# A recommender tower on one core: the products inside two quads joined as sixteen tiles of 32 by 32, and the sums' bank from the common ring

## The chip, the cores and the metric

The kernel runs on one core of a Trainium2 chip. The metric is the device time in microseconds of one execution. A run of the kernel gives one time; the number before the change is the median of three runs.

## What is computed

For each of 512 samples, forty embedding rows of 32 numbers are looked up in forty tables (1,000 to 125,000 rows). Every pair of fields i < j gives one number z = v_i . W_ij . v_j, with a 32 by 32 matrix for each of the 780 pairs. The 780 numbers and 16 context numbers go through three dense layers (796 to 512 to 256 to 1). All is float32.

```
vi = embeddings[:, _I_IDX, :]
vj = embeddings[:, _J_IDX, :]
z = jnp.einsum('bke,kef,bkf->bk', vi, W, vj)
h = jnp.concatenate([z, dense_ctx], axis=1)
h = jnp.maximum(h @ W_top1 + b_top1, 0.0)
h = jnp.maximum(h @ W_top2 + b_top2, 0.0)
y = h @ W_top3
```

## The kernel before

The forty fields stand in ten quads of four fields; a quad fills 128 partitions (four slots of 32), with the 512 samples along the free axis: `emb[:, q, :]`. Quads 0, 1, 3 and 5 ("hot") have small tables. They are looked up on TensorE: ids are spread over the partitions (`spread`, L554), one-hots are made by VectorE (L485) or ScalarE (L405, L408), and multiplied with the table in three bf16 pieces (L572). The other six are gathered by POOL with 96 indirect DMAs (L381), 16 a quad, and turned by TensorE (`turn`, L585). ScalarE copies each finished quad to `emb` (`land`, L415 and L418).

A group (slots, stream) joins two quads. TensorE multiplies each slot's 32 rows of the stream quad with the weights of its four pairs (`map_group`, L600). For two different quads (45 cross groups) these are four row groups of 32, each with two column halves of 64: 8 products of 32 by 64, that go to four banks, a bank for each row group. A group inside one quad (ten) has 4 products of 64 by 64 into two banks. Every float32 product is two instructions, so 16 and 8. Two banks of results are one operation; there are 100 operations, two for each cross group and one for each group inside a quad. An operation is multiplied with the slots' quad, two banks at a time (`multiply`, L316): by VectorE straight from PSUM, or, if it is in COPIED_OPS, from a copy that ScalarE makes (L429), or, if it is in POOL_OPS, by POOL from such a copy. The results go to a ring of eight in SBUF (`prod`). For two operations at a time, TensorE adds up the 32 partitions of each slot with a selector (`sum_ops`, L617): four column groups of 32 with four different streams, 8 instructions, into one bank, `z_ps`. Sixteen operations fill a z tile, which ScalarE copies to `zt` (`save_z`, L433); the sums of the next tile wait for that copy. There are seven z tiles. The first dense layer is added up in parts (`layer1`, L626) as z tiles are ready, its last part, the second layer (L667) and the third (L673) are the tail.

PSUM has eight banks: seven in a ring (`ring_ps`), one for `z_ps`. Orders are written out by hand as strings, one letter a step. TENSOR_ORDER: i spread, l look-up, t turn, m map group, s sum, 1 dense layer. VECTOR_ORDER: r pieces of a table, o one-hot, w multiplication, a addition of a dense part. SCALAR_ORDER: I ids to 16 bits, o one-hot, L landing of a quad, c copy, z copy of a z tile, 1 dense part. BANKS has a digit for each use of the ring, in TensorE's order; a pair is that bank and the next. Before a step, TensorE waits until the last users of its banks are done (`banks_free`). POOL's own queue holds the 96 gathers and then its multiplications.

Of the kernel before, what the change touches and what calls it, by code (L numbers as in the profile page):

```python
# [23 lines left out]
ALU = mybir.AluOpType  # L24
# [26 lines left out]
def quads():  # L51
# [3 lines left out]
    for vocab in HOT_VOCABS:  # L55
# [17 lines left out]
GROUPS = [(slots, stream) for stream in range(QUADS) for slots in range(stream + 1)]  # L73
PAIRS_WITHIN = [(1, 0), (2, 0), (3, 1), (0, 3), (1, 2), (2, 3)]
OPS = [(g, half) for g, (slots, stream) in enumerate(GROUPS) for half in range(1 if slots == stream else 2)]
NOPS = len(OPS)
OPS_OF = [[o for o, (of, _) in enumerate(OPS) if of == g] for g in range(len(GROUPS))]
# [10 lines left out]
RING_BANKS = 7  # L88
# [12 lines left out]
TENSOR_ORDER = ("iillllllilllilllllmllmmtlllmlsllslmlllmmssmsmmstslmlllmlslmlllmmlsmssmssmstmsmsmm1mssmssm1mstmmsmssm"  # L101
                "1msmsm1mstmsmmssmssm1mssm1mssm1mtmmssmssm1mssmssms1m11msssmm1s")


BANKS = ("0240624304042065202024024024660240240240240206420242064024026403042402460242026406204024020640241422"
         "4642604204246024024604320402462301")

VECTOR_ORDER = ("rooooorooooooooooroowwwwooowworwwwwwwwwwooowwwowowwwwwwwwwwwwwwwwwwwwwwwwwwwwwwwwwwwwwwwwwwwwwwwwwww"
                "wwwawwwwaawwwwwawwwwwwwaawawwwa")


SCALAR_ORDER = ("IIoIIIIILIoLoLooLooLooozLcccLzc1cLcc1zc1c1ccLcczcccccLcccczcccczc")
# [47 lines left out]
def bank_users():  # L160
# [597 lines left out]
```

## Time and profile before

| | us |
|---|---|
| median of three runs | 187.92 (187.42 to 188.01) |
| the profiled execution, its own time | 187.37 |
| its span, first to last instruction | 185.6 |
| TensorE busy | 173.7 |
| VectorE busy | 148.1 |
| POOL busy | 114.6 |
| ScalarE busy | 91.9 |

The profiled execution took 1.8 us more than its span. A busy time is the time in which at least one instruction of the engine ran. The pieces of the chain of waits cut TensorE's overlapping instructions at the start of the next piece, so they add up to the time that passes.

### The profile page before, as it was taken

The page shows a single profiled execution, that of the slowest core. Times are in us where ns is not written, and L with a number is a line of the kernel's source. Part 1 is how long each engine was busy: PE and PEld are TensorE (multiplying, and loading weights), DVE is VectorE, ACT ScalarE, POOL GpSimd, SP SyncE. Part 2 cuts the span into 40 slices and gives each one's busy share as a digit, 9 for nine tenths or more (in the row PEclk, how much of TensorE's full clock was granted, in tenths as well). Part 3 has the DMA queues.
Part 4 walks back from the last instruction along what each step waited for, and adds up shares of the span by engine and source line. Part 5 has one row for each costly group of instructions (what it writes and reads, how often), then busy time and mean ns, then how long its engine had stood idle before and what let it go on. Part 6 is the DMA issues. An engine that isn't in the chain of part 4 may idle for free.

```text
span 185.6 us, 4607 instructions
## 1 busy us (share of the span) xinstructions
PE 173.7 (94%) x1976; PEld 47.5 (26%) x1976; DVE 148.1 (80%) x141; ACT 91.9 (50%) x83; POOL 114.6 (62%) x107
## 2 busy tenths in 40 slices
PE   2899979998999999999999899999999899999993
PEld 0243323321333222122221122222221122223331
DVE  0999979998999788997898989888957859981500
ACT  4966999979599521530351533432453342130511
POOL 2877877787877777787777878788096370531000
PEclk9999999999999999999999999999999999999999
DMA  5999400000000019500100000000000000000000
GB/s 173 374 395 359 168 14 16 14 14 14 16 14 16 18 24 350 175 12 11 18 13 16 14 15 15 11 14 14 4 4 0 4 0 4 0 0 4 0 4 0
DMA packets 7212, 10.80 MB, mean 58 GB/s; under 512 B 2052, under 2 KB 4744, under 8 KB 7192
## 3 DMA queue, kind: packets, MB, share of 16 engines
q1 hardware_dynamic: 4088, 8.89, 13.2%
q0 software_dynamic: 3072, 1.58, 4.8%
q8 instruction: 16, 0.26, 0.6%
q10 hardware_dynamic: 32, 0.03, 0.1%
q14 instruction: 4, 0.03, 0.1%
HBM read 10.50 MB, written 0.00 MB: 57 GB/s over the span
## 4 chain that ended last, share of the span: by engine, by line
PE 85%; DVE 5%; ACT 5%; issue 2%; DMA 2%; SPq 0%; DVEq 0%; ACTq 0%
PE ring_ps L600 31%; PE z_ps L617 22%; PE ring_ps L626 14%; PE ring_ps L572 12%; PE ring_ps L667 4%; DVE prod L316 3%; DMA table<-hot_table 2%; ACT copied L429 2%; PE ring_ps L585 2%; ACT distance L405 1%; PE ring_ps L554 1%; ACT one_hot L408 1%; DVE rest L471 1%; DVE one_hot L485 0%; ACT h L463 0%
## 5 line engine op out<-in xcount | busy, mean ns | idle before, releaser
L381 POOL DMA_INDIRECT rows<-table,idx x96 | 97.8, 1019 | 31.7 <-issue 28.9
L316 DVE TENSOR_TENSOR prod<-ring_ps,emb 128x1024 f32<-128x1024 f32 x73 | 86.8, 1219 | 12.1 <-PE ring_ps L600 11.4
L600 PE MATMUL ring_ps<-emb,wall 32*64 32x512 f32 (+1 forms) x800 | 60.6, 612 | 4.4 <-DVE prod L316 2.5
L429 ACT ACTIVATE copied<-ring_ps 128x1024 f32<-128x1024 f32 x27 | 27.6, 1024 | 54.7 <-PE ring_ps L600 51.8
L617 PE MATMUL z_ps<-prod,consts_sb 128*32 128x512 f32 x400 | 49.9, 600 | 0.1
L316 DVE TENSOR_TENSOR prod<-copied,emb 128x1024 f32<-128x1024 f32 x20 | 26.5, 1330 | 5.0 <-ACT copied L429 5.0
L316 POOL TENSOR_TENSOR prod<-copied,emb 128x1024 f32<-128x1024 f32 x7 | 16.6, 2375 | 21.2 <-ACT copied L429 21.2
L626 PE MATMUL ring_ps<-zt,w_sb 128*32 128x512 f32 x224 | 26.7, 597 | 0.0
L600 PEld LDWEIGHTS ring_ps<-emb,wall 32*64 32x64 f32 (+1 forms) x800 | 12.9, 130 | 44.4 <-issue 22.4
L405 ACT ACTIVATE distance<-ids,vocab 128x2048 f16<-128x2048 f16 x10 | 20.0, 2000 | 0.8 <-PE ring_ps L572 0.2
L408 ACT ACTIVATE one_hot<-distance,vocab 128x2048 bf16<-128x2048 f16 x10 | 20.0, 2003 | 0.3
L617 PEld LDWEIGHTS z_ps<-prod,consts_sb 128*32 128x32 f32 x400 | 9.8, 108 | 34.3 <-issue 20.1
L485 DVE TENSOR_SCALAR one_hot<-ids,vocab 128x2048 bf16<-128x2048 f16 x26 | 17.9, 745 | 0.0
L572 PE MATMUL ring_ps<-one_hot,table 128*32 128x512 bf16 x144 | 14.9, 403 | 0.6 <-DVE one_hot L485 0.6
L572 PE MATMUL ring_ps<-one_hot,rest 128*32 128x512 bf16 x144 | 14.9, 400 | 0.0
L572 PE MATMUL ring_ps<-one_hot,third 128*32 128x512 bf16 x144 | 14.8, 398 | 0.0
L626 PEld LDWEIGHTS ring_ps<-zt,w_sb 128*32 128x32 f32 x224 | 6.6, 109 | 18.5 <-issue 16.1
L393 ACT ACTIVATE ids<-ring_ps 128x1024 f16<-128x1024 f32 x8 | 7.8, 1019 | 4.4 <-PE ring_ps L554 4.4
L554 PE MATMUL ring_ps<-ids_rows 16*128 16x512 f16 x16 | 5.8, 500 | 3.7 <-ACT ids_rows L444 3.5
L471 DVE TENSOR_TENSOR rest<-table 128x1024 f32<-128x1024 f32 (+1 forms) x4 | 5.4, 1351 | 4.8 <-DMA table<-hot_table 4.8
L433 ACT ACTIVATE zt<-z_ps 128x512 f32<-128x512 f32 x6 | 3.6, 595 | 7.5 <-PE z_ps L617 7.5
L572 PEld LDWEIGHTS ring_ps<-one_hot,table 128*32 128x32 bf16 x144 | 4.1, 100 | 12.5 <-issue 5.3
(25 smaller groups left out, 56.4 us busy)
## 6 DMA issues: line engine op xcount, KB each, us to landing
w_sb<-w SPq DMA_DIRECT2D x4, 512.0 KB, 5.1
rows<-table,idx POOLq DMA_INDIRECT x96, 2.3
table<-hot_table SPq DMA_DIRECT2D x2, 640.0 KB, 5.9
table<-hot_table SPq DMA_DIRECT2D x2, 512.0 KB, 3.8
wall<-w_pairs SPq DMA_DIRECT2D x1, 640.0 KB, 11.3
wall<-w_pairs SPq DMA_DIRECT2D x1, 576.0 KB
wall<-w_pairs SPq DMA_DIRECT2D x1, 512.0 KB, 8.4
wall<-w_pairs SPq DMA_DIRECT2D x1, 448.0 KB
```

The lines of the kernel that those rows point to most:

```text
L316: return eng.tensor_tensor(prod[:, o % RING_P], products, emb[:, slots:slots + 1, :].to_broadcast([P, 2, BATCH]), ALU.mult)
L381: nc.gpsimd.indirect_dma_start(rows[:, k, c, r, :], None, tables[f], bass.IndirectOffsetOnAxis(ap=idx[:, c, f:f + 1], axis=0)).then_inc(ga ...
L393: nc.scalar.activation(ids16[:, h, 2 * half:2 * half + 2, :], pair(("spread", h), half), ACT.Copy).then_inc(ids16_done, 1)
L405: nc.scalar.activation(distance[:], ids16[:, h].rearrange("p r b -> p (r b)"), ACT.Abs, bias=vocab_column(h, t, -1)).then_inc(distance_don ...
L408: nc.scalar.activation(one_hot[:, n % RING_ONE_HOT, :], distance[:], ACT.Relu, bias=vocab[:, 4 * MAX_TILES:], scale=-1.0).then_inc(one_hot ...
L429: nc.scalar.activation(copied_op(o), op_banks(o), ACT.Copy).then_inc(copied_ready, 1)
L485: nc.vector.tensor_scalar(one_hot[:, n % RING_ONE_HOT, :], ids16[:, h].rearrange("p r b -> p (r b)"), vocab_column(h, t), None, ALU.is_equ ...
L554: mm = nc.tensor.matmul(pair(("spread", h), r // 2)[:, r % 2, :], column, ids_rows[:, :BATCH], start=True, stop=True)
L572: mm = nc.tensor.matmul(bank(("hot", (h, 0)))[DIM * r:DIM * (r + 1), :], shaped[:, r, t, :], one_hot[:, n % RING_ONE_HOT, r * BATCH:(r + 1 ...
L600: mm = nc.tensor.matmul(pair(("map", g), i // 2)[half, i % 2, :], wall[own, g, half], emb[own, stream, :], start=True, stop=True)
L617: mm = nc.tensor.matmul(z_ps[DIM * g:DIM * (g + 1), :], sel[:, m, :], prod[:, t // 2 % RING_P, t % 2, :], start=m == 0, stop=last)
L626: mm = nc.tensor.matmul(bank[DIM * c:DIM * (c + 1), :], w1_sb[:, k, first:first + DIM], zt[:, k, :], start=start and k == ks[0], stop=stop ...
```

## The change

The ten groups inside a quad become five, each for two neighbouring quads (0 and 1, 2 and 3, and so on), with stream = the second one. A joined group has two operations, one for each quad, so 100 operations stay; each operation has two banks of four blocks of 32 by 32, six of them pairs and two with zero weights. All sixteen blocks of a joined group have their own place in the array; a bank takes blocks from two to four row groups. The joined group waits for both quads. The group (0, 0), which only needed quad 0, is gone, so the first map group is (0, 1). The weights' load for stream 0 is gone too (`load_weights`), and those that follow bring only what is left, 50 groups instead of 55.

The separate bank of the sums becomes the eighth of the ring. Each z tile takes a bank by its own digit in BANKS, and its first sum waits for that bank's last user; whoever takes a z tile's bank later waits for its copy to `zt`. Pairs have a digit for each bank now and need not be neighbours.

The four orders, the banks, and the lists of operations on POOL (four instead of seven), of copies (20 as before, beside POOL's) and of ScalarE's one-hots (ten as before) are new.

```diff
-GROUPS = [(slots, stream) for stream in range(QUADS) for slots in range(stream + 1)]
-PAIRS_WITHIN = [(1, 0), (2, 0), (3, 1), (0, 3), (1, 2), (2, 3)]
-OPS = [(g, half) for g, (slots, stream) in enumerate(GROUPS) for half in range(1 if slots == stream else 2)]
+GROUPS = [(slots, stream) for stream in range(1, QUADS) for slots in range(stream + stream % 2)]
+BLOCKS_WITHIN = [[[(0, 0), (1, 0), (2, 0), (3, 1)], [(0, 3), (1, 2), (2, 3), (3, 3)]],
+                 [[(0, 1), (1, 3), (2, 2), (3, 0)], [(0, 2), (1, 1), (2, 1), (3, 2)]]]
+OPS = [(g, half) for g in range(len(GROUPS)) for half in range(2)]
 NOPS = len(OPS)
-OPS_OF = [[o for o, (of, _) in enumerate(OPS) if of == g] for g in range(len(GROUPS))]
+OPS_OF = [[2 * g, 2 * g + 1] for g in range(len(GROUPS))]
...
-RING_BANKS = 7
+RING_BANKS = 8
...
-TENSOR_ORDER = ("iillllllilllilllllmllmmtlllmlsllslmlllmmssmsmmstslmlllmlslmlllmmlsmssmssmstmsmsmm1mssmssm1mstmmsmssm"
-                "1msmsm1mstmsmmssmssm1mssm1mssm1mtmmssmssm1mssmssms1m11msssmm1s")
-
-
-BANKS = ("0240624304042065202024024024660240240240240206420242064024026403042402460242026406204024020640241422"
-         "4642604204246024024604320402462301")
-
-VECTOR_ORDER = ("rooooorooooooooooroowwwwooowworwwwwwwwwwooowwwowowwwwwwwwwwwwwwwwwwwwwwwwwwwwwwwwwwwwwwwwwwwwwwwwwww"
-                "wwwawwwwaawwwwwawwwwwwwaawawwwa")
-
-
-SCALAR_ORDER = ("IIoIIIIILIoLoLooLooLooozLcccLzc1cLcc1zc1c1ccLcczcccccLcccczcccczc")
-
-POOL_OPS = [77, 78, 80, 85, 87, 93, 98]
-COPIED_OPS = [28, 32, 34, 37, 45, 47, 48, 54, 56, 60, 62, 64, 67, 69, 73, 75, 81, 84, 89, 92]
-SCALAR_ONE_HOTS = [4, 17, 21, 23, 25, 27, 30, 31, 34, 35]
+TENSOR_ORDER = ("iiillllllillllllllllmmtsllmlllmlllllsmssmsmsmtllmlssmlllmlllssmlsmsmsmsmsmtsmm1mssmssmsmtsm1mssm1mmm"
+                "ssm1mssmtsmssmssm1mssm1m1mstmssm1mssmmsm1sms1mssms1mssm1s")
+
+
+BANKS = ("0123456701235670142345670132534670134670145670145670135346701346701734012345014523450145230164523670"
+         "1345672014567014501745673014567015236701456723501674672301237670123674012375601235670156723017562301"
+         "6750123236701457234560123601452345601234501762345")
+
+VECTOR_ORDER = ("rooooooooroooooooorowwwoowowowwwrwwwwwwowoowwwowowwwwwwwwwwwwwwwwwwwwwwwwwwwwwwwwwwwwwwwwwwwwwwwwwww"
+                "wawawwawwwwwwawwwwwwwawwwwawwawwwa")
+
+
+SCALAR_ORDER = ("IIIoIIIoLoLIILooLooLooozLcccLzcccL1z11ccccc1LzcccLcccczccccccz")
+
+POOL_OPS = [74, 85, 93, 94]
+COPIED_OPS = [25, 27, 29, 35, 36, 43, 53, 55, 56, 59, 61, 73, 76, 77, 78, 80, 83, 87, 88, 90]
+SCALAR_ONE_HOTS = [4, 10, 16, 20, 25, 26, 27, 33, 34, 35]
...
+def slots_quad(o):
+
+    g, half = OPS[o]
+    slots, stream = GROUPS[g]
+    return stream - 1 + half if within(g) else slots
...
-        if kind == "sum" or kind == "hot" and what[1]:
+        if kind == "sum":
+            if what % GROUP:
+                continue
+            step = "z", what // GROUP
+        if kind == "hot" and what[1]:
             continue
-        size = 2 if kind in ("spread", "map") else 1
-        uses = 2 if kind == "spread" else len(OPS_OF[what]) if kind == "map" else 1
-        banks[step] = [digits.pop(0) for _ in range(uses)]
-        own = [(i, bank) for i, low in enumerate(banks[step]) for bank in range(low, low + size)]
-        before[step] = list(dict.fromkeys(last[bank] for _, bank in own if bank in last))
-        for i, bank in own:
-            last[bank] = (step, i)
+        banks[step] = [digits.pop(0) for _ in range(2 * 2 if kind in ("spread", "map") else 1)]
+        before[step] = list(dict.fromkeys(last[bank] for bank in banks[step] if bank in last))
+        for i, bank in enumerate(banks[step]):
+            last[bank] = (step, i // 2)
...
-            return ring_ps[:, banks[step][i]:banks[step][i] + 2, :]
+            first, second = banks[step][2 * i:2 * i + 2]
+            return ring_ps[:, first:second + 1:second - first, :]
...
-            load_weights(0)
...
-                nc.scalar.activation(zt[:, k, :], z_ps[:], ACT.Copy).then_inc(z_saved, 1)
+                nc.scalar.activation(zt[:, k, :], bank(("z", k)), ACT.Copy).then_inc(z_saved, 1)
...
+                    elif kind == "z":
+                        pe.wait_ge(z_saved, what + 1)
...
-                    pe.wait_ge(landed, landings(stream))
+                    pe.wait_ge(landed, max(landings(q) for q in range(stream + 1)))
                 banks_free(("map", g))
-                height = P // 2 if slots == stream else DIM
-                for i in range(P // height):
-                    own = slice(height * i, height * (i + 1))
+                if within(g):
+                    for half in range(2):
+                        for i, blocks in enumerate(BLOCKS_WITHIN[half]):
+                            for s, r in blocks:
+                                to, own = slice(DIM * s, DIM * (s + 1)), slice(DIM * r, DIM * (r + 1))
+                                mm = nc.tensor.matmul(pair(("map", g), half)[to, i, :], wall[own, g, to],
+                                                      emb[own, stream - 1 + half, :], start=True, stop=True)
+                        mm.then_inc(mapped, 1)
+                    return
+                for i in range(SLOTS):
+                    own = slice(DIM * i, DIM * (i + 1))
                     for c in range(2):
-                        half = slice(P // 2 * c, P // 2 * (c + 1))
-                        mm = nc.tensor.matmul(pair(("map", g), i // 2)[half, i % 2, :], wall[own, g, half],
+                        to = slice(P // 2 * c, P // 2 * (c + 1))
+                        mm = nc.tensor.matmul(pair(("map", g), i // 2)[to, i % 2, :], wall[own, g, to],
                                               emb[own, stream, :], start=True, stop=True)
                     if i % 2:
...
-                    if t % ZTILE == 0 and k:
-                        pe.wait_ge(z_saved, k)
+                    if t % ZTILE == 0:
+                        banks_free(("z", k))
                     last = m == GROUP - 1 or t >= TILES - SLOTS
-                    mm = nc.tensor.matmul(z_ps[DIM * g:DIM * (g + 1), :], sel[:, m, :],
+                    mm = nc.tensor.matmul(bank(("z", k))[DIM * g:DIM * (g + 1), :], sel[:, m, :],
```

## Rows read from the trace of the kernel before

**Rows 1.** Totals of the page: busy time, share of the span, instructions.

```profile
span 185.6 us, 4607 instructions
PE 173.7 (94%) x1976; PEld 47.5 (26%) x1976; DVE 148.1 (80%) x141; ACT 91.9 (50%) x83; POOL 114.6 (62%) x107
```

**Rows 2.** The chain of waits, shares of the span by engine and by line.

```profile
PE 85%; DVE 5%; ACT 5%; issue 2%; DMA 2%; SPq 0%; DVEq 0%; ACTq 0%
PE ring_ps L600 31%; PE z_ps L617 22%; PE ring_ps L626 14%; PE ring_ps L572 12%; PE ring_ps L667 4%; DVE prod L316 3%; DMA table<-hot_table 2%; ACT copied L429 2%; PE ring_ps L585 2%; ACT distance L405 1%; PE ring_ps L554 1%; ACT one_hot L408 1%; DVE rest L471 1%; DVE one_hot L485 0%; ACT h L463 0%
```

**Rows 3.** Stretches: length, busy us of PE, PEld, DVE, ACT, POOL, granted clock, DMA.

```profile
24.92:64.00 39.08, 38.12 (x517) 11.78 (x519) 35.75 (x35) 34.33 (x21) 30.10 (x30) 1.00 0.08 15
64.00:136.00 72.00, 70.88 (x781) 16.14 (x781) 64.65 (x56) 23.14 (x27) 52.28 (x51) 1.00 0.17 46
136.00:169.00 33.00, 31.73 (x344) 7.59 (x340) 23.99 (x21) 11.81 (x13) 15.08 (x7) 1.00 0.00 1
```

**Rows 4.** Groups by line, shapes apart: count, busy us, mean ns, idle before.

```profile
L316 DVE TENSOR_TENSOR prod<-ring_ps,emb 128x1024 f32<-128x1024 f32 x73 | 86.8, 1219 | 12.1 <-PE ring_ps L600 11.4 <-ACT emb L415 0.3 <-PE z_ps L617 0.3
L617 PE MATMUL z_ps<-prod,consts_sb 128*32 128x512 f32 x400 | 49.9, 600 | 0.1
L316 DVE TENSOR_TENSOR prod<-copied,emb 128x1024 f32<-128x1024 f32 x20 | 26.5, 1330 | 5.0 <-ACT copied L429 5.0
L600 PEld LDWEIGHTS ring_ps<-emb,wall 32*64 32x64 f32 x720 | 10.8, 129 | 37.3 <-issue 19.4 <-DVE prod L316 13.7 <-ACT copied L429 4.2
```

**Rows 5.** Pieces of the chain of waits: start us, us, what, instructions.

```profile
81.91 1.85 PE z_ps L617 x16
...
90.60 1.00 PE z_ps L617 x8
...
92.18 2.06 PE ring_ps L600 x24
...
95.25 1.04 PE ring_ps L600 x16
```

**Rows 6.** Timeline (start, us, what): a cross group's weight loads; three multiplications.

```profile
66.86 0.23 PEld L600 LDWEIGHTS ring_ps<-emb,wall 32*64 32x64 f32 x16 [0.84 <-DVE prod L316]
...
26.14 3.49 DVE L316 TENSOR_TENSOR prod<-ring_ps,emb 128x1024 f32<-128x1024 f32 x3 [1.07 <-PE ring_ps L600]
```

**Rows 7.** Timeline of the first stage: ScalarE, TensorE and SP's queue.

```profile
4.53 1.94 ACT L393 ACTIVATE ids<-ring_ps 128x1024 f16<-128x1024 f32 x2 [1.12 <-PE ring_ps L554]
6.57 2.00 ACT L405 ACTIVATE distance<-ids,vocab 128x2048 f16<-128x2048 f16 x1
8.61 2.00 ACT L408 ACTIVATE one_hot<-distance,vocab 128x2048 bf16<-128x2048 f16 x1
...
24.20 0.58 ACT L415 ACTIVATE emb<-ring_ps 128x512 f32<-128x512 f32 x1
...
24.92 2.14 PE L600 MATMUL ring_ps<-emb,wall 32*64 32x512 f32 x24 [1.13 <-ACT emb L415]
26.99 0.66 PE L585 MATMUL ring_ps<-consts_sb,rows 128*128 128x128 f32 x4
...
2.61 0.91 SPq L348 DMA_DIRECT2D wall<-w_pairs  x2
```

**Rows 8.** The last gather, the gathers' time to landing, and the last turn.

```profile
129.02 0.95 POOL L381 DMA_INDIRECT rows<-table,idx  x1 [0.30 <-issue]
...
DMA to landing us min/median/max: 2.2/2.3/3.3
...
135.98 0.66 PE L585 MATMUL ring_ps<-consts_sb,rows 128*128 128x128 f32 x4
```

**Rows 9.** Timeline of the end of the steps.

```profile
163.01 2.13 PE L600 MATMUL ring_ps<-emb,wall 32*64 32x512 f32 x24
...
165.42 2.40 POOL L316 TENSOR_TENSOR prod<-copied,emb 128x1024 f32<-128x1024 f32 x1 [4.41 <-ACT copied L429]
...
167.96 1.07 PE L617 MATMUL z_ps<-prod,consts_sb 128*32 128x512 f32 x8
```

More of the change, by code:

```diff
@@ L97, with within @@
 TAIL = (5, 6)
[L101 to L116 removed]
+TENSOR_ORDER = ("iiillllllillllllllllmmtsllmlllmlllllsmssmsmsmtllmlssmlllmlllssmlsmsmsmsmsmtsmm1mssmssmsmtsm1mssm1mmm"
[9 more added lines that the diff above has]
+SCALAR_ONE_HOTS = [4, 10, 16, 20, 25, 26, 27, 33, 34, 35]
+def within(g):
+    slots, stream = GROUPS[g]
+    return slots == stream
+def slots_quad(o):
+    g, half = OPS[o]
+    slots, stream = GROUPS[g]
+    return stream - 1 + half if within(g) else slots
 def z_place(t):
@@ L286, in op_banks @@
             return pair(("map", g), half)
-        others = [i for i in range(RING_BANKS) if i not in [banks["tail", m][0] for m in range(M1)]]
+        taken = [banks["z", ZTILES - 1][0]] + [banks["tail", m][0] for m in range(M1)]
+        others = [i for i in range(RING_BANKS) if i not in taken]
         h2_ps = [ring_ps[:, others[m], :] for m in range(M2)]
@@ L347, in load_weights @@
                 first = GROUPS.index((0, q))
-                sp.dma_start(wall[:, first:first + q + 1, :].rearrange("p g n -> p (g n)"),
-                             w_pairs[:, first * P:(first + q + 1) * P]).then_inc(wload[q], 16)
+                end = first + q + q % 2
+                sp.dma_start(wall[:, first:end, :].rearrange("p g n -> p (g n)"),
+                             w_pairs[:, first * P:end * P]).then_inc(wload[q], 16)
             sp.dma_start(idx[:].rearrange("p c f -> p (c f)"), ids).then_inc(ids_loaded, 16)
@@ L488, in weight_op @@
             def weight_op(o):
-                slots, _ = GROUPS[OPS[o][0]]
-                dve.wait_ge(landed, landings(slots))
+                dve.wait_ge(landed, landings(slots_quad(o)))
                 if o >= RING_P:
@@ L518, in _ @@
             dve.wait_ge(summed, NOPS // 2)
-            nc.vector.tensor_tensor(zt[:, ZTILES - 1, :], z_ps[:], ctx_sb[:], ALU.add).then_inc(last_z_saved, 1)
+            nc.vector.tensor_tensor(zt[:, ZTILES - 1, :], bank(("z", ZTILES - 1)), ctx_sb[:], ALU.add).then_inc(last_z_saved, 1)
             for m in range(M1):
@@ L686, in packed_weights @@
     for g, (slots, stream) in enumerate(GROUPS):
-        of = PAIRS_WITHIN if slots == stream else [(s, r) for s in range(SLOTS) for r in range(SLOTS)]
-        for s, r in of:
-            packed[r, :, g, s] = block(QUAD_FIELDS[slots][s], QUAD_FIELDS[stream][r])
+        if within(g):
+            of = [(stream - 1 + half, stream - 1 + half, s, r) for half in range(2) for blocks in BLOCKS_WITHIN[half]
+                  for s, r in blocks if s != r]
+        else:
+            of = [(slots, stream, s, r) for s in range(SLOTS) for r in range(SLOTS)]
+        for first, second, s, r in of:
+            packed[r, :, g, s] = block(QUAD_FIELDS[first][s], QUAD_FIELDS[second][r])
     return packed.reshape(P, len(GROUPS) * P)
@@ L699, in packed_layer1 @@
             k, col, m = z_place(2 * o + i)
-            if slots == stream:
-                pairs = PAIRS_WITHIN[3 * i:3 * (i + 1)]
+            if within(g):
+                pairs, of = [(s, r) for s, r in BLOCKS_WITHIN[half][i] if s != r], stream - 1 + half
             else:
-                pairs = [(s, 2 * half + i) for s in range(SLOTS)]
+                pairs, of = [(s, 2 * half + i) for s in range(SLOTS)], stream
             for s, r in pairs:
-                a, b = sorted((QUAD_FIELDS[slots][s], QUAD_FIELDS[stream][r]))
+                a, b = sorted((QUAD_FIELDS[slots_quad(o)][s], QUAD_FIELDS[of][r]))
                 packed[k, DIM * col + SLOTS * m + s] = w[pair_index(a, b)]
```

3 lines of the change are left out of this document (1 added, 2 removed).

## The prediction, made before the change was run

> **What bounds the kernel now.** I read the totals first, then the chain of waits, then the pieces of that chain, and last the stretches. The totals show TensorE busy for 173.7 of 185.6 us and VectorE for 148.1 [rows 1]. The chain puts 85% of the span on TensorE and 5% on VectorE; by line, the block products (L600) have 31% and the sums (L617) 22% [rows 2]. So time is won where TensorE's own steps become fewer or shorter, as long as the engines that feed it keep up. By stretches, TensorE is busy 38.12 of 39.08 us from 24.92, 70.88 of 72.00 from 64 and 31.73 of 33.00 from 136, while VectorE has 35.75, 64.65 and 23.99 there, that is 91%, 90% and 73% [rows 3]. VectorE is therefore the next bound, some 10 points behind. Its idle time is mostly TensorE's doing: 11.4 us of waiting for block products [rows 4], which shrinks when TensorE gets faster.
>
> **Part 1: the products inside a quad.** Every f32 product is two instructions. A cross group has 8 products, 16 instructions; they take 1.04 us. A chain piece with 24 instructions, one cross group and one group inside a quad, takes 2.06 us [rows 5]. So a group inside a quad, with half the products, costs 2.06 - 1.04 = 1.02 us: as much as a whole cross group. Two sums in a row are four passes over 512 columns and take 1.85 us, one ahead of another shape 1.00 [rows 5]: 0.85 for the first, so 0.43 a pass and about 0.15 for a change of shape. Either map group is thus two passes plus 0.16 to 0.18 us, however many tiles stand side by side. The change drops ten such groups: -10.2 us.
>
> It adds five groups of 16 products, 32 instructions. No row shows sixteen tiles of 32 by 32. Below, they can't beat two passes, about 1.02 us. Issue adds little: the 16 weight loads of a cross group begin and end within 0.23 us, one lasting 0.129 [rows 4], so they follow each other at (0.23 - 0.13)/15 = 7 ns [rows 6]. Eight more tiles in each pass start 8 x 7 = 56 ns later, and only the last pass shows that fully: 1.04 + 0.06 = 1.10 us. Above, if only eight tiles run at once, there are two more passes: 1.04 + 0.86 = 1.9 us. Rival B has what lies beyond. I take 1.10, because the rows show that each of its ingredients already runs side by side: four row groups at once (the cross groups), and four column groups with four different streams (the sums). 5 x 1.10 = 5.5 us, so part 1 is worth **-4.7 us**; the bounds are -5.1 and -0.7.
>
> **Part 2: the order.** Counting letters, the sums (49 in the order, one in the tail), cross groups (45), look-ups (36), layer-1 steps (12) and turns (6) stay as they were. Three cross groups now directly follow another cross group. Each such pair saves one change of shape: 3 x 0.16 = **-0.5 us**; at worst nothing.
>
> At the start, the third spread goes ahead of the look-ups, into time in which TensorE waits for the first one-hot anyway. The first cross group now needs quads 0 and 1 landed, and the copy of quad 1 stands behind three of ScalarE's one-hots instead of two. From the first id copy at 4.53 us, six id copies at 0.97, three one-hots at 2 x 2.0 and the copy of quad 0 at 0.55 make 4.5 + 5.8 + 12.1 + 0.55 = 23.0; the copy of quad 1 ends at 23.6 and the first cross group starts at about 23.7, where it was 24.92 [rows 7]. Cross and joined group bring the first turn to 23.7 + 1.04 + 1.10 = 25.85 against 26.99 [rows 7]: 1.1 earlier, just what the dropped groups up to there give. The wider issue on SP (the 64 KB load for stream 0 is gone, some 0.45 us of SP's queue [rows 7]) brings later loads forward by that; the look-ups cover that, for the first cross group waits for ScalarE's copy and not for its weights [rows 7]: zero.
>
> **Part 3: VectorE, POOL, ScalarE.** The 100 multiplications stay, but four instead of seven are POOL's, so VectorE gets three more at about 1.14 us (three in a row take 3.49, one 1.22) [rows 4, 6]: +3.4 us on an engine with room. Up to the last turn VectorE has no more to do than before: about 75 of its operations against 77. Behind it, it has some 21 instead of 16, so 23.99 + 5 x 1.14 = 29.7 us in a stretch that I put at 31 us. That is tight, and is rival A. ScalarE copies 24 instead of 27 tiles, off the path, zero; it is 11.81 us busy in those 33 [rows 3], and would have to be three times as slow to matter.
>
> **Part 4: the sums' bank.** Before, the first sum of a z tile waits for the copy of the last one out of the only bank; now it waits for whoever had its new bank. The waiting instruction holds TensorE's queue, so all later products stand behind it. All 400 instructions of the sums together stood only 0.1 us behind an idle TensorE [rows 4], so the gain is zero. The cost could be a late bank: the ring has eight, the sums hold one, so seven are left, as now. Pairs need no longer be neighbours, so fewer waits, if any. Zero, with half a microsecond on both sides. VectorE reads two banks with a gap between them; its 1.219 us for neighbours and 1.330 us for a copy in SBUF [rows 4] are the nearest bounds (the second would be +0.1 on each of 76, mostly hidden). I take no change: same elements, two runs of 512.
>
> **The gathers.** POOL issues them as before, and the last begins at 129.02 and lands 2.3 us later, at 131.3 [rows 8]. The last turn, at 135.98 now [rows 8], would come at 135.98 - 8 x 1.02 + 4 x 1.10 - 0.5 - 1.04 = 130.7 (the last term is the cross group of quads 7 and 8, which moves behind the turn). So it waits to 131.3: **+0.6 us**. TensorE's waits for VectorE may grow by that much before it and cost nothing. What follows the turn is two old groups inside quads less and one cross and one joined group more, 2.14 against 2.04: no difference (part 1 has it in its count).
>
> **At the end** the second-last multiplication was POOL's: it began at 165.42 and took 2.40, and the last sums started at 167.96 [rows 9]. The last map step ended at 163.01 + 2.13 = 165.14 [rows 9], 2.8 us ahead of them. Now VectorE does both of the last group's, 2 x 1.14 behind the product, some 2.5 us: as long, if VectorE has nothing left over. Zero.
>
> **Sum:** -4.7 - 0.5 + 0.6 = -4.6 us. The profiled execution took 187.37 us, with a span of 185.6 [rows 1]; it would take 182.8. It stood 0.55 under the median of 187.92, so the forecast for the median is 187.92 - 4.6 = **183.3 us**.
>
> **Rivals.**
> A. *VectorE becomes the bound.* For: 91% busy from 24.92 to 64 now, three more operations, and about 29.7 of 31 us behind the last turn. Against: its idle time was TensorE's doing, and the sums without idle time leave 1 to 2 us. If half the gain turns into waits of TensorE for banks and products, -2.3 us: 185.6, between 185.0 and 187.3.
> B. *One bank, several row groups.* In a cross group each row group writes a bank of its own. In the joined group a bank takes four column groups from two to four different row groups. No row shows that. If the array allows a bank only one row group at a time and keeps the order of issue, the listed blocks fall into nine waves: 9 x 0.86 + 0.18 = 7.9 us a group, +29 us in all, 217 us. It decides from the third wave: three give 5 x 2.76 - 10.2 - 0.5 = +3.1 us, so 191.0; two give 1.9 a group, -0.7 - 0.5 = -1.2 us, and 186.7. Against it: within each column group the sixteen blocks go to four different banks, one for each row group, so no 32 partitions of a bank ever get two results at once.
> The Trainium skill, TensorEngine Tiling (Array Packing), Restrictions and Gotchas, states that different row tiles cannot access the same PSUM bank simultaneously. By that rule rival B would hold; the cross groups here keep to it, so the trace neither bears it out nor refutes it.
> C. *The change does not do what it says.* If the sixteen tiles run as two sets of eight, the second bound of part 1, the time is that of two waves, 186.7.
>
> **Chances.** Forecast, 182.0 to 185.0: 0.65. A: 0.16. Two waves (B or C), 186 to 188: 0.06. B from three waves: 0.06. An order whose waits cost more than the groups save, 188.5 to 190: 0.03. More than 6 us gained, if TensorE's waits in the middle go as well: 0.04. A measurement here tells 0.3%, 0.56 us, from no change. Faster by more: 0.65 + 0.04, 0.14 of A and 0.02 of the two waves, 0.85. Within: the other 0.02 of A and 0.04 of the two waves, 0.06. Slower: 0.06 + 0.03 = 0.09. The range runs from 181.9, 1.4 under the forecast, to 186.2, past the middle of A. It leaves out the upper part of A (0.03), the waves (0.12) and the order that costs (0.03), just under 2 in 10.
>
> **What would show it.** Right: five groups at 1.1 us with 32 instructions of 32 by 32 where ten with 8 took 1.02; the first cross group near 23.7; the last turn at 131.3 to 132, just behind the last gather; VectorE's share of busy time up from 80% to 83 or 84%, the end of the chain unchanged. Wrong: a joined group of 1.9 us or more (B, C); or groups of 1.1 us with TensorE's waits for products and banks grown by 2 us and more (A); or a last turn that comes before 131.3, by which the gathers would not be as they were.

## The result, and the profile after

The changed kernel takes **185.76 us** (median of four, 185.27 to 186.13) where the kernel before took 187.96 beside it on the same chip (187.42 to 188.25): a ratio of 0.9894 [0.9874, 0.9913], 2.0 us less by the ratio, 2.2 by the medians. The forecast was 4.6 less. The time lies in the range, close to rival A's 185.6, and the direction was right; more than half of the gain is missing. The profiled execution took 185.81, with these totals and this chain of waits (columns as in [rows 1] and [rows 2]).

```profile
span 184.0 us, 4760 instructions
...
PE 170.3 (93%) x2056; PEld 47.0 (26%) x2056; DVE 149.7 (81%) x144; ACT 88.7 (48%) x80; POOL 108.6 (59%) x104
...
PE 80%; DVE 8%; ACT 7%; issue 2%; DMA 1%; DVEq 0%; ACTq 0%
```

TensorE's busy time fell by 3.4 us and the span by 1.6. The chain shows who took the rest: TensorE's share is down from 85 to 80%, VectorE's up from 5 to 8, ScalarE's from 5 to 7 [rows 2].

**The joined groups cost what was forecast.** Timelines of TensorE (start us, us, line, what), at the first turn and at the second joined group; L618 is a joined group, L626 a cross group, L603 a turn:

```profile
24.72 1.12 PE L626 MATMUL ring_ps<-emb,wall 32*64 32x512 f32 x16 [1.73 <-ACT emb L432]
26.44 1.15 PE L618 MATMUL ring_ps<-emb,wall 32*32 32x512 f32 x32 [0.60 <-ACT ids L410]
27.52 0.66 PE L603 MATMUL ring_ps<-consts_sb,rows 128*128 128x128 f32 x4
...
47.56 1.15 PE L618 MATMUL ring_ps<-emb,wall 32*32 32x512 f32 x32 [0.50 <-DVE prod L333]
48.64 0.55 PE L603 MATMUL ring_ps<-consts_sb,rows 128*128 128x128 f32 x3
```

From one start to the next, 27.52 - 26.44 and 48.64 - 47.56, a joined group of 32 instructions takes 1.08 us, against 1.10 in the sum. What failed is what surrounds it: both groups above stood behind a wait, 0.60 and 0.50 us.

**Where the time went** shows best in the starts of the same steps in the two profiled executions:

| step (start, us) | before | forecast | after |
|---|---|---|---|
| first look-up | 8.12 | | 8.72 |
| first cross group | 24.92 | 23.7 | 24.72 |
| first turn (quad 2) | 26.99 | 25.85 | 27.52 |
| cross group of quads 0 and 6 | 77.89 | | 78.57 |
| turn of quad 7 (one layer-1 step fewer ahead of it after) | 91.53 | | 91.38 |
| last turn (quad 9) | 135.98 | 131.3 | 135.38 |
| span | 185.6 | | 184.0 |

Two of these places in the timelines, the cross group of quads 0 and 6 and the turn of quad 7, first before, then after (before, the cross group is the second part of a piece of 24 instructions and starts at 76.87 + 1.02 = 77.89):

```profile
76.87 2.13 PE L600 MATMUL ring_ps<-emb,wall 64*64 64x512 f32 x24
...
91.53 0.66 PE L585 MATMUL ring_ps<-consts_sb,rows 128*128 128x128 f32 x4
```

```profile
78.57 1.13 PE L626 MATMUL ring_ps<-emb,wall 32*64 32x512 f32 x16
...
91.38 0.66 PE L603 MATMUL ring_ps<-consts_sb,rows 128*128 128x128 f32 x4
```

At the cross group of quads 0 and 6, six old groups have become three joined ones: 6 x 1.02 - 3 x 1.10 = 2.8 us of the forecast. All other steps ahead of it are the same in number. Yet it starts 0.7 us later than before. From there to the end the kernel is 2.3 us shorter; the four old groups made two joined ones there are 4 x 1.02 - 2 x 1.10 = 1.9. So the late part paid about as forecast, 0.7 of it at the very end, where none was forecast (see "The end" below), and the first part paid nothing.

By stretches (length; busy us of PE, PEld, DVE, ACT, POOL; granted clock; DMA), first the kernel before, then the changed one:

```profile
24.00:64.00 40.00, 38.12 (x517) 11.81 (x519) 36.67 (x35) 35.25 (x23) 30.85 (x31) 1.00 0.08 15
64.00:79.00 15.00, 14.67 (x168) 3.40 (x172) 13.59 (x12) 4.05 (x5) 11.35 (x12) 1.00 0.54 173
79.00:136.00 57.00, 56.21 (x618) 12.75 (x617) 51.06 (x45) 19.09 (x22) 40.93 (x40) 1.00 0.08 13
136.00:165.00 29.00, 27.84 (x308) 6.42 (x300) 21.77 (x19) 11.48 (x13) 12.67 (x6) 1.00 0.01 1
```

```profile
24.00:64.00 40.00, 37.19 (x556) 12.31 (x560) 36.70 (x36) 32.39 (x21) 30.55 (x32) 1.00 0.09 15
64.00:79.00 15.00, 13.76 (x176) 3.11 (x176) 13.88 (x13) 4.87 (x6) 11.64 (x12) 1.00 0.52 171
79.00:136.00 57.00, 55.36 (x641) 13.07 (x625) 49.82 (x45) 15.91 (x19) 42.60 (x41) 1.00 0.07 13
136.00:165.00 29.00, 28.50 (x341) 6.49 (x344) 25.91 (x24) 11.72 (x13) 7.12 (x3) 1.00 0.01 2
```

TensorE's idle time grew by 0.93, 0.91 and 0.85 us in the first three stretches (38.12 - 37.19, and so on) and fell by 0.66 in the last. The stretch with most idle time for its length is the second: TensorE idles 1.24 of 15 us while VectorE is busy 13.88. Its timeline:

```profile
67.32 1.23 DVE L333 TENSOR_TENSOR prod<-copied,emb 128x1024 f32<-128x1024 f32 x1
67.33 1.12 PE L626 MATMUL ring_ps<-emb,wall 32*64 32x512 f32 x16 [0.30 <-ACT copied L446]
...
68.56 1.03 ACT L446 ACTIVATE copied<-ring_ps 128x1024 f32<-128x1024 f32 x1 [1.38 <-PE ring_ps L626]
68.57 1.22 DVE L333 TENSOR_TENSOR prod<-ring_ps,emb 128x1024 f32<-128x1024 f32 x1
...
69.72 1.23 DVE L333 TENSOR_TENSOR prod<-copied,emb 128x1024 f32<-128x1024 f32 x1
69.74 1.12 PE L626 MATMUL ring_ps<-emb,wall 32*64 32x512 f32 x16
```

A cross group comes every 69.74 - 67.33 = 2.41 us, though it takes 1.04 and the sum beside it 1.00 [rows 5], together 2.04. Two things hold it, and they are equally long. VectorE has two multiplications for each group and does them back to back: 67.32, 68.57, 69.72. And the next group needs two banks that this one had: it ends at 68.45, ScalarE copies its second half out from 68.56 to 69.59, and at 69.74 the next starts. Three pairs of banks make a ring in which each engine waits for the other.

### The profile page after: what moved, and what is told of

The parts are those of the page before. It is cut to its first block, busy times and chain, and to the rows that moved or that the text cites. A ratio compares the mean times of both kernels' runs of the same rounds, so it can differ in the third digit from the quotient of the medians.

```text
span 184.0 us, 4760 instructions
## 1 busy us (share of the span) xinstructions
PE 170.3 (93%) x2056; PEld 47.0 (26%) x2056; DVE 149.7 (81%) x144; ACT 88.7 (48%) x80; POOL 108.6 (59%) x104
## 4 chain that ended last, share of the span: by engine, by line
PE 80%; DVE 8%; ACT 7%; issue 2%; DMA 1%; DVEq 0%; ACTq 0%
PE ring_ps L643 21%; PE ring_ps L626 21%; PE ring_ps L652 14%; PE ring_ps L590 11%; DVE prod L333 8%; PE ring_ps L693 4%; PE ring_ps L572 3%; PE ring_ps L618 3%; ACT distance L422 2%; ACT one_hot L425 2%; PE ring_ps L603 2%; ACT copied L446 1%; DMA ids_sb<-hot_ids 1%; ACT ids L410 1%; ACT h L480 0%
## 5 line engine op out<-in xcount | busy, mean ns | idle before, releaser
L333 DVE TENSOR_TENSOR prod<-ring_ps,emb 128x1024 f32<-128x1024 f32 x76 | 90.0, 1217 | 11.3 <-PE ring_ps L626 10.7
L626 PE MATMUL ring_ps<-emb,wall 32*64 32x512 f32 x720 | 49.9, 611 | 4.4 <-DVE prod L333 1.8
L643 PE MATMUL ring_ps<-prod,consts_sb 128*32 128x512 f32 x400 | 50.0, 599 | 1.2 <-ACT copied L446 0.5
L446 ACT ACTIVATE copied<-ring_ps 128x1024 f32<-128x1024 f32 x24 | 24.2, 1024 | 40.2 <-PE ring_ps L626 32.1
L333 DVE TENSOR_TENSOR prod<-copied,emb 128x1024 f32<-128x1024 f32 x20 | 24.8, 1255 | 1.4 <-ACT copied L446 1.4
L333 POOL TENSOR_TENSOR prod<-copied,emb 128x1024 f32<-128x1024 f32 x4 | 10.1, 2532 | 20.9 <-ACT copied L446 20.9
L626 PEld LDWEIGHTS ring_ps<-emb,wall 32*64 32x64 f32 x720 | 11.1, 129 | 39.3 <-issue 19.1
L643 PEld LDWEIGHTS ring_ps<-prod,consts_sb 128*32 128x32 f32 x400 | 10.0, 108 | 33.4 <-DVE prod L333 19.0
L450 ACT ACTIVATE zt<-ring_ps 128x512 f32<-128x512 f32 x6 | 3.6, 594 | 16.2 <-PE ring_ps L643 16.2
L435 ACT ACTIVATE emb<-ring_ps 128x512 f32<-128x512 f32 x6 | 3.6, 599 | 12.5 <-PE ring_ps L603 12.5
```

The lines of the kernel that those rows point to most:

```text
L333: return eng.tensor_tensor(prod[:, o % RING_P], products, emb[:, slots:slots + 1, :].to_broadcast([P, 2, BATCH]), ALU.mult)
L446: nc.scalar.activation(copied_op(o), op_banks(o), ACT.Copy).then_inc(copied_ready, 1)
L626: mm = nc.tensor.matmul(pair(("map", g), i // 2)[to, i % 2, :], wall[own, g, to], emb[own, stream, :], start=True, stop=True)
L643: mm = nc.tensor.matmul(bank(("z", k))[DIM * g:DIM * (g + 1), :], sel[:, m, :], prod[:, t // 2 % RING_P, t % 2, :], start=m == 0, stop=last)
```

## Experiments

"Held together" in the expectations is this theory: TensorE, VectorE, ScalarE and the pairs of banks between them stand within a microsecond of each other, so what TensorE saves turns into waits; and a turn can't start before its gather has landed. V and T, in the expectations of 1 to 3, are explained in the first of them. All times of runs are medians; ratios are to the kernel before, measured beside them. Where two runs are compared that were not measured beside each other, the difference is taken from their ratios; the changed kernel's is 0.9894. The four runs of 1 to 3 were made before the others.

**1. TensorE shorter in the first part, in both kernels.** The look-ups' third piece is left out:

```
- for k, piece in enumerate([first_piece(h), second_piece(h), third[:, h % RING_HOT, :width(h)]]):
+ for k, piece in enumerate([first_piece(h), second_piece(h)]):
```

> The changed kernel, but every look-up multiplies two of a table's three pieces; the third is still made by VectorE and left out of the result. TensorE has 36 x 0.22 = 7.8 us less to do ahead of 64 us, no other engine has less. Theory V (up to about 75 us VectorE's own work and its waits set the pace, so that TensorE's savings there are worth little): 0 to 1 us faster than the changed kernel, 184.8 to 185.8. Rival T (TensorE sets the pace throughout, and the gain was lost in TensorE's own waits at two places of the new order): 3 us faster or more, up to where the gathers hold it, 183 or less.

> The same cut (third piece of each table left out of the look-ups) in the kernel before. Both theories say that TensorE was nearer to being the bound there: V expects 1 to 3 us faster than the kernel before, T 3 us or more.

Measured: the changed kernel 185.08, ratio 0.9826 [0.9776, 0.9875], so some 1.3 us under the changed kernel whole; the kernel before 187.59, ratio 0.999 [0.9957, 1.0023], no gain that stands out from the noise, where both theories expected 1 us or more.

The clock took part of the saving. TensorE, with less to do, stood longer ahead of the first cross group, and the clock then fell: the kernel before with shorter look-ups, 20 to 24 and 24 to 28 us (columns as above), and its first map groups and first turn:

```profile
20.00:24.00 4.00, 1.82 (x24) 0.34 (x16) 3.97 (x4) 3.97 (x4) 3.09 (x4) 1.00 0.15 39
24.00:28.00 4.00, 3.87 (x25) 0.79 (x26) 3.15 (x4) 3.88 (x2) 3.09 (x4) 0.57 0.07 12
```

```profile
24.13 3.78 PE L600 MATMUL ring_ps<-emb,wall 32*64 32x512 f32 x24 [2.32 <-ACT emb L415]
27.84 0.66 PE L585 MATMUL ring_ps<-consts_sb,rows 128*128 128x128 f32 x4
```

At a mean granted clock of 0.57, most of that stretch at the lower level of 1.2 GHz, the two groups took 27.84 - 24.13 = 3.71 us, against 26.99 - 24.92 = 2.07 [rows 7]. Three of this kernel's ten executions kept a mean clock of 1.00 over the whole run: 187.10 to 187.19, 0.9 under the kernel before. Of the four of the changed kernel with shorter look-ups, one did: 184.08, 1.6 under the median of the changed kernel's three executions at 1.00 (185.72). So 7.8 us less of TensorE's work are worth 0 to 1.6 us, even where the clock held. Already in the kernel before, TensorE alone did not set the pace up to 64 us, for all its 38.12 busy of 40 us.

**2. VectorE lighter in the first part.** Multiplications 8 to 33 do the first bank alone:

```
+ if 8 <= o < 34:
+     return eng.tensor_tensor(prod[:, o % RING_P, :1], products[:, :1],
+                              emb[:, slots:slots + 1, :], ALU.mult)
```

> The changed kernel, but the multiplications 8 to 33 are made for the first of their two banks only (the second half of their products is left as it was in the ring): 26 x about 0.5 us less for VectorE between 37 and 78 us, TensorE unchanged. V: 1.5 us faster than the changed kernel or more, 184.3 or less. T: under 0.7 us faster, 185.1 or more.

Measured: 184.66, ratio 0.9816 [0.9777, 0.9854], 1.5 us less by the ratios for 13 us of VectorE's time; it lies between the bounds of V and T. Between 66 and 74 us the cross groups still came every 2.41 us, now behind ScalarE's copies alone: the ring of banks was the equal second. And the turn of quad 4 stood 0.90 us, until 48.97, for its last gather, which began at 46.48 and with the median landing time of 2.4 us was in at about 48.9. So VectorE alone was not the bound either.

**3. TensorE longer in the first part.** The joined groups of streams 1, 3 and 5 issue their products twice:

```
- for half in range(2):
+ for half, again in [(h, a) for a in range(2 if stream < 6 else 1) for h in range(2)]:
...
- mm.then_inc(mapped, 1)
+ if again == (1 if stream < 6 else 0):
+     mm.then_inc(mapped, 1)
```

> The changed kernel with the products of the joined groups of streams 1, 3 and 5 computed twice: 3 x 0.86 = 2.6 us more on TensorE ahead of 79 us. T: 2.2 to 2.6 us slower than the changed kernel, 188.0 to 188.4. V: slower by less, 0.5 to 1.8 us, as part of it falls into TensorE's waits for VectorE.

Measured: 189.58, ratio 1.0069 [1.004, 1.0098], 1.8% over the changed kernel, some 3.3 us, more than either theory expected. The edit itself was larger than the 2.6 us of the expectation. The first doubled group:

```profile
26.00 2.56 PE L618 MATMUL ring_ps<-emb,wall 32*32 32x512 f32 x64 [0.60 <-ACT ids L410]
28.50 0.66 PE L603 MATMUL ring_ps<-consts_sb,rows 128*128 128x128 f32 x4
```

It takes 28.50 - 26.00 = 2.50 us instead of 1.08; the other two take 2.49 instead of 1.08 and 2.28 instead of 1.12, so TensorE has 4.0 us more. Of 4.0 us more, 3.3 arrive; of 7.8 us less, at most 1.6: the sign of several limits at the same place.

**4. ScalarE lighter.** Its one-hots take one pass instead of two:

```
- nc.scalar.activation(distance[:], ids16[:, h]..., ACT.Abs, bias=vocab_column(h, t, -1))
- nc.scalar.activation(one_hot[:, n % RING_ONE_HOT, :], distance[:], ACT.Relu, ...)
+ nc.scalar.activation(one_hot[:, n % RING_ONE_HOT, :], ids16[:, h]..., ACT.Relu, ...)
```

> The changed kernel with ScalarE's ten one-hots in one pass of 2.0 us instead of two (the pass for the distance is left out): 20 us less on ScalarE, all of it ahead of 64 us. Theory 'held together': alone it gives no more than the shorter look-ups or the lighter VectorE did, 0 to 1 us: 184.8 to 185.8, and the cross group of quads 0 and 6 starts no earlier than 77.5 (78.6 in the changed kernel, 74.2 with three engines relieved). Theory 'ScalarE alone holds the first part': most of the 4.4 us that three relieved engines gave there come from it, the cross group of quads 0 and 6 starts at 75.5 or before.

Measured: 186.75, ratio 0.9905 [0.9871, 0.9938], no gain; the upper end of the forecast missed by a microsecond. Five of its ten executions had a mean clock of 1.00 and took 185.06 to 186.66, with a median of 185.76, the changed kernel's; the other five, at 0.99, took 186.85 to 187.84. The profiled execution, 186.66, is the slowest of the first five. The first joined group started 0.8 us earlier, at 25.66, and the turn behind it then waited 1.9 us for its gather. That gather took 3.94 us to land in the profiled execution (the chain of waits: start us, us, what):

```profile
22.55 1.76 POOL rows L398
24.61 3.94 DMA rows<-table,idx
```

All that follows was about 1 us late to the end. How late this one gather lands, and whether the clock holds, are part of the scatter between runs.

**5. All three lighter, and then the gathers earlier.** The edits of 1, 2 and 4 together; in the second kernel the 16 gathers of quad 4 are left out besides; in the third they alone:

```
- for r, f in enumerate(QUAD_FIELDS[q]):
+ for r, f in enumerate(QUAD_FIELDS[q] if k != 1 else []):
```

> The changed kernel with three engines relieved together: every look-up leaves out its third piece (TensorE 7.8 us less), VectorE's multiplications 8 to 33 do the first bank alone (13 us less), and ScalarE's one-hots take one pass instead of two. Singly the first two gave 0.7 and 1.1 us. Theory 'held together' (up to the cross group of quads 0 and 6 TensorE, VectorE and ScalarE stand within about a microsecond of each other): relieved together they give more than the sum of the single gains there, that cross group starts at about 75.5 instead of 78.6; but the turn of quad 7 (91.4) can't come before its gather lands (89.9 in the changed kernel), so only 1 to 2 us reach the end: 183.8 to 184.8, and TensorE waits 1 us or more for the gather ahead of that turn. Theory 'TensorE alone' (the prediction's): 185.1, as with the shorter look-ups alone. Theory 'the start' (the loss lies in the waits up to the first turn): the time from the first turn to the cross group of quads 0 and 6 stays at 51 us, and the start alone moves.

> The kernel with three engines relieved together, and besides without the 16 gathers of quad 4 (its turn reads quad 2's rows), so that each later gather lands one gather, about 21 us, earlier. Theory 'held together, with the gather of quad 7 as a floor': what the relieved first part saves now reaches the end, the cross group of quads 0 and 6 starts at 74 to 75.5, the turn of quad 7 follows it without a wait, 3 us or more of gain against the changed kernel: 181 to 183. If gathers are no floor: the same time as the kernel with three engines relieved, within 0.6 us.

> The changed kernel without the 16 gathers of quad 4 alone (its turn reads quad 2's rows). Theory 'held together': with the engines as they are, the gathers are ahead of the turns by more than a microsecond, so no change within 0.6 us of the changed kernel: 185.2 to 186.4. Theory 'the gathers bound the changed kernel' (the floor alone ate the early savings): 1 us or more is gained, 184.8 or less, and the turn of quad 7 comes earlier than 90.4.

Measured: ratios of 0.9818 [0.9767, 0.9869], 0.9591 [0.9546, 0.9635] and 0.987 [0.9835, 0.9905]; the medians of the last two are 181.19 and 185.5. With three engines lighter, the cross group of quads 0 and 6 starts at 74.2, 4.3 us earlier (74.1 in the second kernel), where the single edits gave 0.6, 0.3 and nothing; but the gain ends at the turns, which wait for their gathers. No two of the three were lightened without the third, so how much each adds to the others in the first part is open. The waits of TensorE in the first kernel (us, times, longest; its profiled execution took 186.46, at a mean clock of 0.97):

```profile
PE ring_ps L604 <- DMA rows<-table,idx: 3.7, 2, 2.0
...
PE ring_ps L604 <- DVE prod L336: 2.5, 1, 2.5
```

The second row is the turn of quad 7. VectorE, to which it is put down, had left that bank at 85.8; the turn began at 89.42, when its gather was in. Without quad 4's gathers it starts at 86.8 with no wait, and by the ratios 4.3 us more reach the end; part of these is the clock, which fell behind that wait (last section). Without lighter engines the same early gathers give 0.3 to 0.5 us, within the noise. So the gathers do not hold the changed kernel, but they are a floor just below it: the last gather of quad 4 landed at 48.2, 0.4 us ahead of its turn, that of quad 7 at about 89.9 (87.52 + 2.4), 1.5 us ahead.

**6. The start.** Two places exchanged in ScalarE's order, nothing left out:

```
- "IIIoIIIoLoLIILooLoo..."
+ "IIIoIIoIIILLoLooLoo..."
```

> The changed kernel with two places exchanged at the beginning of ScalarE's order: the copies of the fourth spread's ids stand ahead of the landing of quad 0, and the third one-hot stands behind the landing of quad 1. Nothing is left out. The first cross group waited for the landing of quad 1 (24.7) and the first joined group for those id copies (26.4); now about 23.4 and 24.5. Theory 'the start' (most of what was missing is lost there for good): the 1 to 2 us reach the end, 184.5 or less. Theory 'held together': VectorE and ScalarE's later one-hots take most of it back, 0.3 to 0.8 us reach the end: 185.0 to 185.5.

Measured: 186.32, ratio 0.9896 [0.986, 0.9932], as the changed kernel. TensorE's timeline:

```profile
23.11 1.12 PE L626 MATMUL ring_ps<-emb,wall 32*64 32x512 f32 x16 [0.91 <-ACT emb L432]
24.16 1.21 PE L618 MATMUL ring_ps<-emb,wall 32*32 32x512 f32 x32
27.02 0.63 PE L603 MATMUL ring_ps<-consts_sb,rows 128*128 128x128 f32 x4 [1.65 <-DMA rows<-table,idx]
```

Both groups came 1.6 and 2.3 us earlier, as meant, and the turn waited 1.65 us for the gather instead. The small gain foreseen did not show: the median lies 0.8 us over the forecast, with executions from 185.0 to 188.63. So the late start alone is not what lost the time: behind ScalarE's copies stood the gather of quad 2, whose turn came at 27.02, only 0.5 us earlier than in the changed kernel.

**7. The late part.** Four layer-1 steps between the turns of quads 7 and 9 take one z tile instead of two, 3.5 us less on TensorE; then the same with every multiplication from the ninth on lightened, and that alone (`if 8 <= o:` in the edit of 2):

```
+ few = what in ((0, 1), (0, 2), (0, 3), (1, 0))
- layer1(bank(("layer1", what)), PARTS[part], m).then_inc(lin_done, 1)
+ layer1(bank(("layer1", what)), PARTS[part][:1] if few else PARTS[part], m).then_inc(lin_done, 1)
```

> The changed kernel, in which four of the layer-1 steps behind the turn of quad 7 (at 94.0, 99.8, 108.2 and 122.8) take one z tile instead of two: 4 x 0.88 = 3.5 us less on TensorE in the late part, where the change's savings did arrive. Theory 'held together in the first part, TensorE alone in the late part': up to the turn of quad 7 nothing moves, and behind it the saving arrives until the last turn meets its gather (135.4 against 131.9): 2 to 3.2 us gained, 182.6 to 183.8. Theory 'VectorE bounds the changed kernel throughout': under 1 us, 184.8 or more.

> The changed kernel in which every multiplication from the ninth on, VectorE's and POOL's, does the first bank alone: 0.53 us less on each, some 45 us of VectorE's time. Theory 'VectorE alone bounds the changed kernel' (rival A of the prediction, carried over the whole span): every wait of TensorE behind the first turn goes, 13.8 - 7.7 = 6 us, as far as the last gather lets it: 182 or less. Theory 'held together': TensorE's own work stands just behind, the same 1.1 us as with the lighter multiplications 8 to 33 alone and at most 1.5 us more: 183.2 to 184.7.

> The kernel with every multiplication lightened, and besides with the four shortened layer-1 steps (TensorE 3.5 us less between the turns of quads 7 and 9). With VectorE as it is, these four steps gave 1.0 us, and TensorE's waits for multiplications to free banks rose from 1.8 to 4.1 us. Theory 'held together' (what TensorE saves, VectorE takes, over the whole span): with VectorE out of the way the saving arrives, up to the last gather: 2 us or more below the kernel with lighter multiplications alone. Theory 'the four steps cost TensorE little to begin with, or the gathers took their saving': again 1 us or less.

Measured, in the order of the expectations: 184.72, ratio 0.9817 [0.9768, 0.9866]; 184.49, ratio 0.9819 [0.978, 0.9858]; 181.07, ratio 0.9633 [0.9601, 0.9666]. The first was a miss: I had thought that in the late part TensorE alone decides, and of the 3.5 us only 1.4 arrived (1.0 by the medians; its two executions at a mean clock of 1.00, 183.88 and 184.18, lie 1.7 under the median of the changed kernel). The other two tell why. Light multiplications alone give 1.4 us; with them, the four short steps give 184.49 - 181.07 = 3.4, all of their 3.5. So in the late part, too, the two engines hold each other. The stretch from 91.5 to 135 (columns as above), with the shorter steps alone, and then with both:

```profile
91.50:135.00 43.50, 40.53 (x480) 9.31 (x472) 38.25 (x35) 13.36 (x18) 33.07 (x31) 1.00 0.08 13
```

```profile
91.50:135.00 43.50, 42.89 (x508) 9.89 (x504) 23.21 (x37) 14.71 (x18) 29.84 (x30) 1.00 0.08 13
```

With VectorE as it is, TensorE has 2.97 us of idle time in it; with light multiplications 0.61, although it has the same steps to do. And the waits of TensorE, changed kernel and shorter steps:

```profile
PE ring_ps L626 <- DVE prod L333: 1.8, 5, 0.5
```

```profile
PE ring_ps L626 <- DVE prod L333: 4.1, 9, 0.7
```

In the chain of waits of the kernel with shorter steps the ring is open to the eye:

```profile
97.83 1.15 PE ring_ps L626 x16
98.98 0.03 issue
99.01 1.24 DVE prod L333
100.24 0.14 issue
100.38 1.21 PE ring_ps L626 x16
```

A cross group ends, VectorE takes its half out, and only then are there two banks for the next. Where the layer-1 step between them is 1.85 us long, VectorE's 1.24 hide beneath it; at 1.0 they don't.

None of the runs that do the whole work is faster than the changed kernel.

## Why the prediction was right or wrong

**Right: the price of the joined group** (part 1), 1.08 against 1.10. Rivals B and C are refuted: there are no nine waves and no two sets of eight. The Trainium skill, TensorEngine Tiling (Array Packing), Restrictions and Gotchas, states that different row tiles cannot access the same PSUM bank simultaneously. This trace does not bear it out: a bank took tiles of two to four row groups, each into partitions of its own, and the joined group took 1.08 us, a cross group 1.04.

**Wrong: "So time is won where TensorE's own steps become fewer or shorter"**, the step on which every term of the sum rests. The sentence goes on "as long as the engines that feed it keep up", and the prediction took that as met: VectorE stood some 10 points behind and had room. The -4.7 are TensorE's own time; they were carried to the end one for one, and about 2 us of them and of the order's 0.5 arrived (what the order gave by itself, no run shows). Run 1 shows that the condition already failed in the kernel before: 7.8 us less, under 1 us of gain. The reason given was false as well: that VectorE's idle time "is mostly TensorE's doing", 11.4 us of waits for block products, and shrinks as TensorE gets faster. After the change these waits are 10.7 us. In a ring each engine's waits bear the other's name. TensorE's wait for a free bank and VectorE's wait for the next product are two halves of one turn of the ring, and the page puts each down to whoever came last. The high busy share of TensorE hid that it had no slack to win: 97 to 98% busy beside a VectorE at 91%, and a chain that could run through either. Run 7 shows it plainest, 1.4 us or 3.4 for the same edit.

**Wrong: the gathers' term, +0.6.** It was taken at the last turn alone. The forecast put the first turn at 25.85, when its gather, begun at 23.73 in the kernel before, would land at 23.73 + 2.3 = 26.0. At the turn of quad 7 the gap is larger. The last gather of that quad, in the kernel before:

```profile
86.72 0.94 POOL L381 DMA_INDIRECT rows<-table,idx  x1 [0.30 <-issue]
```

It lands 2.3 us later, at 89.0. The new order has three joined groups for six old ones ahead of this turn and one layer-1 step fewer, 1.85 us, which the prediction did not mention. So by its own prices the turn was to come at 91.53 - 2.8 - 1.85 = 86.9 and to wait 2.1 us; carried on to the last turn, 130.7 + 2.1 = 132.8, that is 2.1 instead of 0.6. By these rows even a TensorE that saved all it was to save would have gained some 3.1 us, not 4.6. In the changed kernel itself the term came out at nothing, because TensorE was late: the last turn came at 135.38, and the last gather, begun at 129.53, landed at 131.8. In run 5 it is this floor that stops the gain.

**Wrong: the first cross group at 23.7** (part 2). It came at 24.72. The chain of ScalarE's operations was added up without its waits; the changed kernel's timeline of ScalarE has two, for look-ups that free a one-hot's buffer:

```profile
14.84 2.00 ACT L422 ACTIVATE distance<-ids,vocab 128x2048 f16<-128x2048 f16 x1 [0.76 <-PE ring_ps L590]
...
19.95 2.00 ACT L422 ACTIVATE distance<-ids,vocab 128x2048 f16<-128x2048 f16 x1 [0.59 <-PE ring_ps L590]
```

The spread moved ahead of the look-ups was costed at nothing, as lying in idle time; the first look-up began 0.6 us later, look-ups ran at half their later pace until 13.8 us instead of 11.9 (last section), and they freed buffers later. By run 6 none of this reached the end.

**Wrong: part 4's "fewer waits, if any".** The new banks brought a few: the first joined group stands 0.60 us for ScalarE's copies of ids, which hold its banks, and a layer-1 step (at 80.20) and the first sum of a z tile (at 147.14) 0.5 us each for a copy out of the bank that they take. Together that is 1.6 us. Other waits for banks shrank; in all they went from 3.1 to 4.2 us, more than the half microsecond allowed. The sums' instructions, 0.1 us behind an idle TensorE before [rows 4], now stand 1.2. Whether VectorE reads two banks with a gap as fast as neighbours stays open: all pairs in the new BANKS are neighbours.

**Rival A** had the right time with half of the right mechanism, so its 185.6 is in part luck. Half the gain did turn into waits of TensorE, for banks above all. But VectorE did not become the bound: its share is 81%, not the 83 to 84 forecast, and 45 us less of its work give 1.4 us. After the change it holds the pace together with TensorE. Before it, run 1 shows only that TensorE did not hold it alone; VectorE was not lightened in the kernel before.

**The end** was forecast at no change; TensorE's idle time between 136 and 165 us fell from 1.16 to 0.50 us. That gave 0.7 back, which no term of the sum had.

## What to carry to other kernels

Two engines that pass a few buffers back and forth are one bound, not a bound and a follower: before a saving on the busier one is carried to the end, find for each step the wait that would come next, and price it. A cheap test on the old kernel, a step with part of its work left out, would have told that 7.8 us less on TensorE bring under 1 us; the clock of such a test is to be looked at too, because TensorE ran at half its pace after the longer wait. And a floor such as a gather's landing is to be set against the forecast at every step that waits for it, in the new order of steps, not at the last alone.

## What the runs showed of the hardware that was not expected

**Sixteen f32 tiles of 32 by 32, four in each bank from two to four row groups, run in 1.08 us**, 0.04 more than eight tiles of 32 by 64.

**A short wait of TensorE can cost more than itself.** Run 1 has one case, at the first map groups. Another: with all three engines lighter, TensorE was busy 1.57 us of the 4.4 ahead of the turn of quad 7; the stretch behind it then ran at a granted clock of 0.50, that is 1.2 GHz:

```profile
85.00:89.40 4.40, 1.57 (x24) 0.27 (x17) 4.37 (x4) 0.67 (x1) 3.18 (x4) 0.88 0.08 11
89.40:94.00 4.60, 4.58 (x28) 1.24 (x28) 0.02 (x1) 1.18 (x2) 3.68 (x4) 0.50 0.11 16
```

One sum there, from 90.44 to 92.30, took 1.86 us, as long as two take elsewhere [rows 5]. The four executions of this kernel had mean clocks of 0.97 to 0.99, so the clock is probably one reason why it gained so little by its ratio, although its first part was 4.3 us shorter. Where VectorE's work is whole, executions at a mean clock of 0.99 were as a rule some 1 us longer than those at 1.00: 186.66 against 185.35 to 185.51 with the early gathers alone, 185.26 and 185.32 against 183.88 and 184.18 in run 7's first kernel.

**At the start, TensorE's pace doubles while the clock's column says 1.00 throughout.** The timeline of the changed kernel, two pieces of a look-up, at 0.42 us from start to start and later at 0.21:

```profile
9.54 0.64 PE L590 MATMUL ring_ps<-one_hot,third 128*32 128x512 bf16 x4
9.97 0.64 PE L590 MATMUL ring_ps<-one_hot,table 128*32 128x512 bf16 x4
...
14.47 0.38 PE L590 MATMUL ring_ps<-one_hot,table 128*32 128x512 bf16 x4
14.69 0.38 PE L590 MATMUL ring_ps<-one_hot,rest 128*32 128x512 bf16 x4
```

Before, it doubled at 11.9 us, after the change at 13.8. So work that is moved into the first microseconds is not to be priced by rows of later work.

**A gather's landing varied**: 2.3 to 2.4 us in the median, 3.17 and 3.94 at the first turn in two runs (6 and 4), and up to 5.9 in the first kernel of run 5.
